# Part of the second projection, normalisation and routing moved into the last steps of the second attention

## The reference, cut to what matters

```python
out = einsum('bhts,bhsd->bhtd', attn, v_enh)          # second attention
x   = x + out @ out_w + out_b                         # its projection
xt  = layernorm(x)                                    # 2048 tokens of 128
logits = xt @ router_w                                # 8 experts
idx = argmax(softmax(logits)); gate = max(softmax(logits))
pos = cumsum(one_hot(idx)) * one_hot(idx) - 1         # place in the expert's queue, kept if < 256
# each token's row goes to row idx*256 + pos of the experts' input
h = relu(expert_inputs @ w1 + b1); y = h @ w2 + b2    # per expert, 256 rows
x = x + gate * y[its row]
```

## Time and profile before

| | |
|---|---|
| median of 3 runs | 1106.92 us (1104.48 to 1108.74) |
| the profiled execution's own time | 1098.76 us |
| its span, first to last instruction | 1096.9 us |
| mean granted TensorE clock | 0.928 |
| busy: TensorE, VectorE, ScalarE, GpSimd | 964.5, 758.0, 593.1, 330.1 us |

### The profile page before, as it was taken

The page is one execution under the profiler, slowest core; times in us unless marked ns, Lnnn a source line. Parts: engine busy times, 40 slices in busy tenths (PEclk is TensorE's granted clock), DMA queues, the critical chain, the costliest instruction groups (busy, mean ns, idle before and its releaser), DMA issues. The chain is left out here.

```text
span 1096.9 us, 18648 instructions
## 1 busy us (share of the span) xinstructions
PE 964.5 (88%) x6220; PEld 627.4 (57%) x6220; DVE 758.0 (69%) x2263; ACT 593.1 (54%) x1165; POOL 330.1 (30%) x417
## 2 busy tenths in 40 slices
PE   6889999999999999999739388889999999997474
PEld 4666666767766767677439355344444444444463
DVE  6766758777676767677533599887888888872523
ACT  4866757666676756567413183415555555555121
POOL 2522112211221111112053207343544344521523
PEclk9999999999999999999859698968999999999587
DMA  6540000000000000000161100000000000000623
GB/s 194 120 126 2 1 1 1 1 1 1 1 1 2 1 1 2 1 2 1 51 184 43 53 0 1 1 1 1 1 2 1 1 2 1 1 1 1 208 59 101
DMA packets 49546, 32.16 MB, mean 29 GB/s; under 512 B 9339, under 2 KB 46124, under 8 KB 49452
## 3 DMA queue, kind: packets, MB, share of 16 engines
q1 hardware_dynamic: 47404, 26.72, 8.6%
q0 software_dynamic: 2048, 4.26, 1.2%
HBM read 21.38 MB, written 11.69 MB: 30 GB/s over the span
## 5 line engine op out<-in xcount | busy, mean ns | idle before, releaser
L562 ACT ACTIVATE attn_a_prob<-attn_a_score,attn_a_m_all 128x128 f32<-128x128 f32 (+7 forms) x256 | 188.9, 741 | 50.8 <-DVE attn_a_m_all L482 46.9
L912 ACT ACTIVATE attn_b_probT<-attn_b_st 128x1024 f32<-128x1024 f32 (+1 forms) x192 | 145.2, 808 | 130.2 <-PE attn_b_st L778 128.8
L478 DVE TENSOR_REDUCE attn_a_m_far<-attn_a_score 128x1 f32<-128x512 f32 (+3 forms) x192 | 105.7, 551 | 78.4 <-PE attn_a_score L390 76.3
L402 PE MATMUL attn_a_slot<-tab,attn_a_prob 128*128 128x128 f32 x1152 | 148.8, 273 | 1.4 <-ACT attn_a_prob L562 1.2
L402 PEld LDWEIGHTS attn_a_slot<-tab,attn_a_prob 128*128 128x128 f32 x1152 | 131.7, 140 | 9.8 <-issue 2.1
L414 PE MATMUL attn_a_o<-attn_a_ptsa,Vd 128*64 128x512 f32 x288 | 136.4, 603 | 0.0
L414 PE MATMUL attn_a_o<-attn_a_ptsb,Vd 128*64 128x512 f32 x288 | 136.4, 603 | 0.0
L841 DVE CUSTOM_DVE_ANT_0 attn_b_slot<-attn_b_slot,later 128x128 f32<-128x128 f32 (+3 forms) x256 | 118.6, 522 | 18.5 <-PE attn_b_slot L753 18.5
L571 ACT ACTIVATE attn_a_ptsa<-attn_a_slot 128x512 f32<-128x512 f32 x144 | 85.9, 597 | 80.5 <-PE attn_a_slot L402 79.8
L753 PE MATMUL attn_b_slot<-KS,attn_b_alone 128*128 128x512 f32 (+2 forms) x384 | 125.3, 423 | 2.9 <-POOL attn_b_alone L934 2.5
L482 DVE CUSTOM_DVE_ANT_0 attn_a_score<-attn_a_score,bias_near,attn_a_m_far 128x256 f32<-128x256 f32 (+2 forms) x192 | 107.4, 559 | 6.8
(11 more groups left out here) (244 smaller groups left out, 1838.3 us busy)
## 6 DMA issues: line engine op xcount, KB each, us to landing
moe_weights_w<-in_L_ffn_w_dram SPq DMA_DIRECT2D x32, 256.0 KB, 5.0
to_experts<-xn SPq DMA_DIRECT2D x2, 1056.0 KB, 11.4
moe_experts_xe<-to_experts SPq DMA_DIRECT2D x16, 132.0 KB, 2.5
bias_by_query_and_key<-bias_by_distance SPq DMA_DIRECT2D x2, 1024.0 KB
bias_near<-bias_by_query_and_key SPq DMA_DIRECT2D x2, 1024.0 KB, 6.2
from_experts<-xn SPq DMA_DIRECT2D x2, 1024.0 KB, 11.4
moe_experts_back<-from_experts SPq DMA_DIRECT2D x8, 256.0 KB, 3.9
X<-in_L_attn_a_x_dram SPq DMA_DIRECT2D x2, 512.0 KB, 4.8
```

The source lines that it names most:

```text
L402: ins = nc.tensor.transpose(dst[:, jj * P:(jj + 1) * P], probs(g)[:, 2 * jj + half, i * P:(i + 1) * P], ident[:, :])
L478: nc.vector.tensor_reduce(least, score[t % 2][:, at:at + nk - win], AX.X, ALU.min).then_inc(far_done, 1)
L562: nc.scalar.activation(probs(g)[:, j, 0:nk], score[t % 2][:, at:at + nk], ACT.Exp, bias=m_all[:, j:j + 1], scale=-1.0, accum_out=rowsum[g ...
L912: nc.scalar.activation(probT[n % 2][:, two, lo:], st[:, two, lo:], ACT.Exp, scale=-1.0).then_inc(exp_done, 1)
```

## The change

Chunks 0 and 1 (the first batch) are projected, normalised, routed and placed inside `attention_b`, in steps 86 to 94. A table `BESIDE` says at which step TensorE does which piece, always at the end of its step. The pieces use the same ring of three banks; `emptied` says which semaphore frees a bank. The layernorm's inverse root is made without ScalarE: GpSimd raises the variance to -0.5, and VectorE refines it twice. GpSimd scatters tiles 0 and 1 (`AHEAD = 2`) during `project_out`, tiles 2 to 7 at the beginning of `dispatch`, and the rest after their chunks are placed. `project_out` and the second `dispatch` do chunks 2 and 3 alone, the latter in the order turn, turn, logits, logits, counts, counts on TensorE and with both square roots ahead. The routing's small tiles move to the room of `woa`, which the first attention has left. In both dispatches `logit` has two banks instead of one; the first is otherwise as it was. The second attention has 11 more semaphores.

```diff
+AHEAD = 2
@@ dispatch(..., route, first, gate, xe_dram, sent, loads)
+        logit = [ph.psum(f"logit{i}", [P, BANK // E, E]) for i in range(2)]
+        parts = (range(0, 2 * BLK), range(2 * BLK, TILES)) if first == 0 else tuple(range(c * BLK, (c + 1) * BLK) for c in CHUNKS)
@@ tensor
+            else:
+                for c in CHUNKS:
+                    turn(c)
+                for c in CHUNKS:
+                    logits(c)
+                for c in CHUNKS:
+                    counts(c)
@@ vector
+            else:
+                variance(1)
+                inverse(0)
+                normal(first)
+                inverse(1)
+                normal(first + 1)
+                for c in CHUNKS:
+                    choose(c)
+                    place(c)
@@ gpsimd
-            for i in range(TILES):
-                if i % BLK == 0:
-                    pool.wait_ge(placed, i // BLK + 1)
-                pool.indirect_dma_start(...)
+            if first:
+                send_tiles(nc, range(AHEAD, first * BLK), route, xn, xe_dram, sent)
+            for c in CHUNKS:
+                pool.wait_ge(placed, nth(c))
+                send_tiles(nc, range(c * BLK, (c + 1) * BLK), route, xn, xe_dram, sent)
@@ attention_b
+    END = STEPS - LAG
+    BESIDE = {END: (("ot", 0),), END + 1: (("y", 0), ("ot", 1)), END + 2: (("y", 1),), END + 5: (("xt", 0),),
+              END + 6: (("xt", 1), ("logit", 0)), END + 7: (("count", 0), ("logit", 1)), END + 8: (("count", 1),)}
+        oT = [xnT[:, 1, 1 + i * BANK:1 + (i + 1) * BANK] for i in range(2)]
+        freed_by = {"ot": oT_ready, "y": summed, "xt": xnT_ready, "logit": ranked, "count": placed}
@@ tensor
+            def project(c):
+                dst = open_slot(slot["y", c])
+                pe.wait_ge(oT_ready, c + 1)
+                for j in range(BLK):
+                    ins = nc.tensor.matmul(dst[:, j * P:(j + 1) * P], oT[c][:, j * P:(j + 1) * P], w_out[:, :], start=True, stop=True)
+                ins.then_inc(slot_filled, 1)
+            def turn_normal(c):
+                pe.wait_ge(xn_ready, c + 1)
+                turn(slot["xt", c], xn[:, c * BLK:(c + 1) * BLK, 0:D])
...
+            beside = {"ot": turn_out, "y": project, "xt": turn_normal, "logit": logits, "count": counts}
...
+                for kind, c in BESIDE.get(n, ()):
+                    beside[kind](c)
@@ vector
+            def inverse():
+                r = route.rstd[:, 0:QT]
+                dve.wait_ge(guessed, 1)
+                for _ in range(2):
+                    link(nc.vector.tensor_tensor(slope[:, :], r, route.var[:, 0:QT], ALU.mult))
+                    link(nc.vector.scalar_tensor_tensor(slope[:, :], slope[:, :], -0.5, r, ALU.mult, ALU.mult))
+                    link(nc.vector.scalar_tensor_tensor(r, slope[:, :], 1.5, r, ALU.add, ALU.mult))
...
+                for kind, c in BESIDE.get(n, ()):
+                    if kind == "y":
+                        add_out(c)
+                        if c == 1:
+                            variance()
+                            inverse()
+                            normal(0)
+                            normal(1)
+                    if kind == "logit":
+                        choose(c)
+                    if kind == "count":
+                        place_tokens(c)
@@ scalar
+                for kind, c in BESIDE.get(n, ()):
+                    if kind in ("ot", "xt"):
+                        u = slot[kind, c]
+                        act.wait_ge(slot_filled, u + 1)
+                        dst = oT[c][:, :] if kind == "ot" else xnT[:, 0, 1 + c * BANK:1 + (c + 1) * BANK]
+                        nc.scalar.activation(dst, bank[u % SLOTS_S][:, :], ACT.Copy).then_inc(freed_by[kind], 1)
@@ gpsimd
+                if n == END + 3:
+                    pool.wait_ge(var_ready, 1)
+                    nc.gpsimd.tensor_tensor(route.rstd[:, 0:QT], route.var[:, 0:QT], half[:, :], ALU.pow).then_inc(guessed, 1)
@@ project_out(..., first, route, xn, xe_dram, sent)
-            turn(0)
-            turn(1)
-            for c in range(NC):
+            for c in CHUNKS:
+                turn(c)
+            for c in CHUNKS:
                 project(c)
-                if c + 2 < NC:
-                    turn(c + 2)
+        @block.gpsimd
+        def _(pool):
+            send_tiles(nc, range(0, AHEAD), route, xn, xe_dram, sent)
```

More of the change, by code:

```diff
@@ new lines, in chunk, with wide, count_places @@
+def chunk(x, c):
+    return x[:, c * BLK:(c + 1) * BLK]
+def wide(x):
+    return x.unsqueeze(2).to_broadcast([P, BLK, E])
+def count_places(nc, route, c, out):
+    nc.tensor.matmul(out, route.upper[:, :], chunk(route.mask_bf, c), start=True, stop=False)
+    for i in range(c * BLK):
+        nc.tensor.matmul(out, route.ones_bf[:, :], route.mask_bf[:, i:i + 1, :].to_broadcast([P, BLK, E]), start=False, stop=False)
+    for s in range(1, BLK):
+        ins = nc.tensor.matmul(out[:, s:BLK, :], route.ones_bf[:, :], route.mask_bf[:, c * BLK:(c + 1) * BLK - s, :], start=False, stop=s == BLK - 1)
+    return ins
@@ L88, in dispatch @@
+def dispatch(nc, name, X, stats, xn, xnT, ident, router, route, first, gate, xe_dram, sent, loads):
     NC = TILES // BLK
+    CHUNKS = range(first, NC)
     with Phase(nc, name) as ph:
[L90 to L93, removed]
@@ L119, in logits @@
             def logits(c):
-                pe.wait_ge(copied, c + 1)
+                pe.wait_ge(copied, nth(c))
                 for i in range(c * BLK, (c + 1) * BLK):
                     at = 1 + (i % QT) * P
-                    ins = nc.tensor.matmul(logit[:, i, :], xnT[:, i // QT, at:at + P], router[:, :], start=True, stop=True)
+                    ins = nc.tensor.matmul(logit[c % 2][:, i, :], xnT[:, i // QT, at:at + P], router[:, :], start=True, stop=True)
                 ins.then_inc(routed, 1)
             def counts(c):
[L129 to L138, removed]
-            turn(0)
-            logits(0)
-            counts(0)
-            turn(1)
[L144 to L148, removed]
+                pe.wait_ge(masked, nth(c))
+                if c >= first + 2:
+                    pe.wait_ge(placed, nth(c) - 2)
+                count_places(nc, route, c, count[c % 2][:, 0:BLK, :]).then_inc(counted, 1)
+            if first == 0:
+                turn(0)
+                logits(0)
+                counts(0)
+                turn(1)
+                for c in range(1, NC):
+                    logits(c)
+                    if c + 1 < NC:
+                        turn(c + 1)
+                    counts(c)
[3 more added lines that the diff above has]
+                for c in CHUNKS:
+                    logits(c)
+                for c in CHUNKS:
+                    counts(c)
         @block.scalar
@@ L164, in _ @@
             deviation(0)
-            copy(0)
-            deviation(1)
-            for c in range(1, NC):
+            if first:
+                deviation(1)
+            copy(first)
+            if not first:
+                deviation(1)
+            for c in CHUNKS[1:]:
                 copy(c)
-            act.wait_ge(ranked, NC)
+            act.wait_ge(ranked, len(CHUNKS))
             nc.scalar.activation(ex[:, :, :], rank[:, :, :], ACT.Exp).then_inc(exped, 1)
@@ new lines, in variance @@
+            def variance():
+                for i in range(QT):
+                    ins = nc.vector.bn_aggr(route.mv[:, i, :], stats[:, i, :])
+                link(ins)
+                nc.vector.memset(half[:, :], -0.5)
+                nc.vector.tensor_scalar(route.var[:, 0:QT], route.mv[:, 0:QT, 1], EPS, None, ALU.add).then_inc(var_ready, 1)
+            def inverse():
[5 more added lines that the diff above has]
+                    link(nc.vector.scalar_tensor_tensor(r, slope[:, :], 1.5, r, ALU.add, ALU.mult))
```

198 lines of the change are left out of this document (138 added, 60 removed).

## The result

The changed kernel took 1094.95 us (median of 4 runs, 1092.17 to 1095.73), the kernel before beside it 1106.25 (4 runs). The ratio is 0.9889, with a 95% interval of 0.9869 to 0.9909. That is 11.3 us faster where 7.6 was forecast. The profiled execution after took 1094.28, its span is 1092.1 and its mean clock 0.935.

A forecast was written before the change was run, and what follows sets the result against it. GpSimd's queue of sixteen scatters was taken to bound the routing stretch. Tail +3.8, projection -3.07, second routing -8.9 and landing +0.6 gave -7.6 us, carried to the median: 1099.3 us, range 1094 to near 1107.

The forecast's parts named there:

- The chain: Last routing stretch: start of the first scatter, plus sixteen times 1.264 us, plus 5.2, sets when the experts start.
- Chunk 2's first scatter: Second routing: comes 10.3 us into the phase, with GpSimd free since 7.7; later than 11 would be wrong.
- The tail: Attention's last steps: TensorE's added pieces cost +3.8 us, from steps 86 to 87, 92, 93 and 94.
- Rival A: Attention's tail eats the gain through TensorE, ScalarE's copies and late landing: 1102 to 1107; 0.18 jointly with C, part of 0.10.
- The power: GpSimd's power in the layernorm chain: 0.5 us, bounds 0.46 and 3.5, with a slack of 1.95; cost 0.
- The projection: Projection phase: two chunks less at VectorE's 1.54 per chunk, -3.07 us; two scatters beside it hidden.
- Landing: End of the scatters: the last two land under the end of the weight loads, +0.6 us, bounds 0 and 3.2.
- Second routing with landing: Last routing stage: scatters issued early end the last one sooner, -8.9 us, with +0.6 for landing.
- the carrying over: Whole kernel: -7.6 us from the profiled 1098.76 gives 1091.2; put on the median 1106.92 it gives 1099.3.
- D: More hides than counted: attention costs 2.2, landing nothing; gain 9.8, 1097 us; 0.63 together with the forecast.
- B: Slow GpSimd power delays step 91, each us above 2.5 adding one; part of 0.10, beyond that part of 0.09.
- C: Scatters do not run ahead, beside the projection phase: 2 to 3 us lost, 1102 us; 0.18 jointly with A.

The follow-up runs named there:

- 7: Changed kernel with a second power of the same size on GpSimd ahead of the first; single run of 1099.86 us.
- 2: Changed kernel, unchanged, with a second profile; 1091.84 us against 1100.29 for the kernel before, ratio 0.9926.
- 6: Changed kernel with the second mixture's weights of experts 4 to 7 loaded in the experts' phase; 1093.58 us, ratio 0.9885.
- 14: Changed kernel with 32 more bf16 products at the beginning of TensorE's list in both dispatches; 1089.63 us, ratio 0.9899.
- 1: Kernel before, unchanged, with a second profile; 1099.69 us, ratio to itself 1.0004.
- 3: Kernel before with only the second logit bank, in both dispatches; 1100.23 us, ratio 1.0006.
- 9: Kernel before, unchanged, once more on a chip of the longer time; 1105.83 us against 1106.38, ratio 0.9998.
- 12: Kernel before with the weights of experts 4 to 7 loaded in the experts' phase in both mixtures; 1106.06 us, ratio 0.9998.
- 15: Kernel before with GpSimd waiting in both dispatches until all four chunks are placed, then 16 scatters; single run of 1125.24 us.
- 16: Kernel before, unchanged, as the control of its job; single run of 1103.61 us.
- 11: Changed kernel, weights of experts 4 to 7 late in both mixtures, second dispatch's TensorE order making chunk 2's counts before chunk 3's logits; 1094.92 us, ratio 0.9895.
- 8: Changed kernel with TensorE making chunk 2's counts ahead of chunk 3's logits in the second dispatch; 1094.33 us, ratio 0.9896.
- 17: Kernel before with 32 more products at the beginning of TensorE's list, on a chip of the longer time; 1106.07 us, ratio 0.9996.
- 18: Changed kernel with TensorE's list shifted by 32 products, on a chip of the longer time; 1094.05 us, ratio 0.9874.

## Why the prediction was right and where it was wrong

*The chain.* Right on the 1100 level: the scatters' queue set the stage's end, and the experts moved with it. Chunk 2's first scatter came 10.50 into the stage (10.3 forecast), though not for the reason worked out. On the 1100 level it comes after 9.6, and on the 1106 level the wait adds 0.9.

*The tail*, forecast 3.8, measured 3.15. Steps 86 and 87 cost 1.93 of 2.16, step 92 0.66 of 0.81, step 93 0.52 of 0.73. Full-width steps with a turn or a projection cost 0, as argued from ScalarE's pace. Rival A fell.

*The power.* 1.69 instead of 0.5, inside its bounds and covered. The slack after it was 0.7; by the prediction's 1.95 with the 1.2 above 0.5 taken off it should have been 0.76. The agreement is partly luck: the rows were ready 0.45 sooner than worked out, and of the 0.6 that was to be free after TensorE asked, only about 0.1 was, because ScalarE's copy lies on the path (7).

*The projection*, forecast -3.07. The phase is 8.85 long before and 5.86 after where both ran at full clock (-2.99), 9.92 and 6.78 where both ran near half clock in the first part, 0.57 and 0.62 (-3.14). Between the first two profiles it is -4.06, since the granted clock was lower there before than after. The clearing of semaphores cost nothing, as forecast (the attention has 11 more, not 15): the phase starts 0.32 after VectorE's last instruction of the attention in both.

*Landing*, forecast +0.6: the load starts 3.40 after the last scatter instead of 2.94 (+0.5). In 2 it is 4.22 (+1.3). Both are above the 3.2 that the prediction named as a sign of being wrong. Without the late loads (6) it is 2.86, and in 14, with them, 3.10.

*Second routing with landing*, forecast -8.9 + 0.6 = -8.3. In 1 and 2 it is -8.2 (34.07 to 25.84). That the sum is right owes something to luck: the last scatter ends 9.5 sooner and the landing takes 1.3 back. On the 1106 level it is -10.5 (36.59 to 26.05).

**The step that failed** is the sentence that chunks 1 to 3 are placed long before GpSimd comes to them, so that before the change the queue of scatters runs without a gap. Already in the trace of the first profile the margins were 0.39, 1.85 and 3.28 us, of which the prediction took no account. On the 1106 level chunk 2 is placed 4.0 later, and the queue stands still for 2.4 us more (first to last scatter 21.6 instead of 19.1). In the changed kernel six scatters that began early end sooner, chunk 2 is held for only 0.9, and 0.2 of the stage is left of it. With this the carrying over failed too: the sum was taken from an execution of 1098.76 and put on a median of 1106.92, as if the 8 us between them lay outside the changed stretch. About 5 of them are two such waits, one per mixture, and the change removes the second.

*The last us.* The sums of these terms are 3.15 - 3.0 - 8.2 = -8.1 where 8.5 was timed, and 3.15 - 3.0 - 10.5 = -10.4 where 11.3 and 11.9 were. The profiles hold most of the rest. From the exponential of step 86 to the start of the routing, the nine profiles with the kernel before's attention and projection take 33.76 to 35.28, mean 34.47; nine of the changed kernel's (without 7) take 32.85 to 34.44, mean 33.49. That is -1.0 where 3.15 - 3.0 makes +0.15. It goes by the granted clock. In five of the nine before (3, 9, 12, 15, 16) steps 88 and 89 together take 1.4 us more. In 9, for example, the clock is 0.50 from 990 to 992, after TensorE had been busy for 1.05 of 2.00 us. In three of the other four the projection is 10.7 to 10.8 long. None of the changed kernel's profiles has this, and TensorE is busy there for 12.45 of 13.00 us from 990 to 1003, against 10.30. That the added work is what keeps the clock up is argued, not shown. The first profile, with 33.76, was the shortest of its nine here as well.

The rivals: on the 1106 level the gain went beyond D's 9.8, but not for D's reasons. Steps 92 and 93 did not hide and the landing cost something. B and C did not occur.

Open stays what makes VectorE wait on some chips. Ruled out are the weight loads (11, 12), the counts' own time (8) and the q8 packet (17). No kernel tried is measurably faster than the change: 6 (0.9885) and 18 (0.9874) lie within its interval, and 14 has no unchanged neighbour to be compared with.

## What to carry to other kernels

Where the one profile in hand is well under the median of the runs, ask which stretch holds the difference before a sum from the one is put on the other; a serial queue in the changed stretch is the first suspect. Before calling a queue gapless, write down each margin with which its inputs are ready: the smallest ones (0.39 and 1.85 us here) say how much delay turns into a gap. Shortening such a queue can also remove the stalls inside it, so it was worth more here than instructions times period. Pieces put beside a loop were free in steps where another engine kept the pace (0 in full-width steps) and cost nearly their whole length in the narrow ones (1.93 of 2.16).

## What the runs showed of the hardware that was not expected

- The same kernel took 1100.0 to 1100.3 us on two chips and 1106.2 to 1106.9 on three others. About 4.8 of the 6 us are two waits before the third chunk's placing (VectorE waits 3.2 to 4.6 us in each), and in the last stage ScalarE's next copy is late too.
- GpSimd's power on 128x8 elements took 1.69 us, a second one right behind it 1.63.
- The rows' load started 4.22 after the last scatter in 2 and 3.10 in 14, though both issued that scatter 18.4 us into the stage, under the same weight loads.
- A packet of 16 KB of the kind "instruction" came on queue q8 once in each routing stage. It moved with 32 products added to TensorE's list (1034.0 to 1019.0) without any effect on the time of the kernel before (0.9989 and 0.9996).
- The granted clock fell at different points of the attention's last steps and of the projection in equal kernels: the projection before was 8.85 to 10.74 long, and steps 88 and 89 of the attention took 1.4 us more in five of nine profiles.
